# A cross-attention and mixture-of-experts layer: routed tiles in pairs, with a split down projection

## The reference

```python
x = x + xattn(layernorm(x), k, bias, ctx, ctx, num_heads=8)   # causal convolution over the features, per head
n = layernorm(x).reshape(2048, 256)
scores = softmax(n @ Wg.T)                                    # 16 experts in 4 groups
# the 2 best groups, then the 4 best experts of them; combine = their scores
h = silu(einsum('td,eid->eti', n, W1)) * einsum('td,eid->eti', n, W3)     # 176 hidden features
y = einsum('etd,te->td', einsum('eti,edi->etd', h, W2), combine)
z = (silu(n @ Ws1.T) * (n @ Ws3.T)) @ Ws2.T                   # shared expert, 352 hidden
out = x + y + z
```

## Time and profile before

| | |
|---|---|
| median of 3 runs | 452.86 us (450.76 to 453.48) |
| the profiled execution | 448.65 us, span 446.9 us |
| TensorE matmul (PE) busy | 420.3 us, 94% |
| VectorE (DVE) busy | 231.1 us, 52% |
| ScalarE (ACT) busy | 178.7 us, 40% |
| POOL busy | 185.3 us, 41% |
| chain that ended last | PE 83%, DMA 6%, DVE 3%, issue 3% |
| granted TensorE clock, mean | 0.996 |

### The profile page before, as it was taken

One profiled execution on the slowest core, in us unless ns is written; L12 is line 12 of the kernel. 1 busy time (PEld: TensorE's weight loads), 2 busy tenths in 40 slices (PEclk: granted clock), 3 DMA queues, 4 the chain that ended last, 5 costly groups with the idle time before them and its releaser, 6 DMA issues.

```text
span 446.9 us, 9516 instructions
## 1 busy us (share of the span) xinstructions
PE 420.3 (94%) x2197; PEld 303.5 (68%) x2198; DVE 231.1 (52%) x635; ACT 178.7 (40%) x522; POOL 185.3 (41%) x232
## 2 busy tenths in 40 slices
PE   0799999999899999998899999999999998999797
PEld 0678778877678455655666777777777776676576
DVE  2457668988877557384324343343333333333275
ACT  4335656644554531110243443444444443444221
POOL 3125233254887667752033333433433333333240
PEclk9999999999999999999999999999999999999989
DMA  7989999889989356544223333333333332334998
GB/s 196 271 214 245 232 231 226 229 205 273 306 233 319 139 163 244 200 172 149 55 93 105 100 112 113 109 115 100 111 114 103 109 112 89 111 100 126 338 385 312
DMA packets 47497, 79.97 MB, mean 179 GB/s; under 512 B 6017, under 2 KB 37233, under 8 KB 45425
## 3 DMA queue, kind: packets, MB, share of 16 engines
q1 hardware_dynamic: 40560, 59.74, 48.3%
q0 software_dynamic: 6912, 19.93, 11.4%
HBM read 55.12 MB, written 24.55 MB: 178 GB/s over the span
## 4 chain that ended last, share of the span: by engine, by line
PE 83%; DMA 6%; DVE 3%; issue 3%; ACT 2%; POOL 1%; DVEq 1%; POOLq 0%; ACTq 0%
PE heads L1120 19%; PE bank L1177 14%; PE heads L1032 11%; PE heads L1155 9%; PE heads L1034 6%; PE bank L1167 5%; PE heads L1130 4%; DMA y_scratch<-toep,dest_i 4%; PE bank L1143 3%; PE bank L1046 3%; PE bank L1239 2%; DMA ctx_n<-ctx_in 2%; PE bank L1057 2%; PE bank L1073 1%; DVE kv L639 1%
## 5 line engine op out<-in xcount | busy, mean ns | idle before, releaser
L622 POOL DMA_INDIRECT y_scratch<-toep,dest_i x80 | 77.5, 969 | 151.7 <-ACT toep L469 138.0
L1120 PE MATMUL heads<-w,toep 128*128 x320 | 111.1, 469 | 2.2 <-ACT toep L457 1.1
L1177 PE MATMUL bank<-w,toep 88*128 x320 | 83.5, 384 | 0.0
L1032 PE MATMUL heads<-toep,kv 128*128 128x256 f32 x256 | 79.8, 394 | 2.8 <-DVE kv L639 2.8
L1120 PEld LDWEIGHTS heads<-w,toep 128*128 128x128 f32 x320 | 56.7, 190 | 33.7 <-issue 12.0
L927 DVE COPY toep<-toep 128x1 f32 x77 | 11.8, 154 | 120.2 <-DMA y_scratch<-toep,dest_i 115.8
L571 POOL DMA_INDIRECT rows_scratch<-rows,slot_i x64 | 62.9, 983 | 21.6 <-issue 20.2
L1177 PEld LDWEIGHTS bank<-w,toep 88*128 88x128 f32 x320 | 54.9, 191 | 5.0
L653 DVE TENSOR_TENSOR prod<-heads,ctx_rep 128x1024 f32<-128x1024 f32 x32 | 39.2, 1224 | 30.0 <-PE heads L1034 29.6
L1034 PEld LDWEIGHTS heads<-toep,kv 128*128 128x128 f32 x256 | 49.8, 195 | 7.1
L463 ACT ACTIVATE toep<-heads 128x176 f32<-128x176 f32 x80 | 25.4, 317 | 71.3 <-PE heads L1120 71.3
(11 more groups left out here) (188 smaller groups left out, 454.5 us busy)
## 6 DMA issues: line engine op xcount, KB each, us to landing
ctx_rep<-ctxr_in SPq DMA_DIRECT2D x16, 1024.0 KB, 7.5
toep<-rows_scratch SPq DMA_DIRECT2D x77, 144.0 KB, 2.1
w<-w_in SPq DMA_DIRECT2D x16, 352.0 KB
w<-w_in SPq DMA_DIRECT2D x16, 176.0 KB
rows_scratch<-pad_row SPq DMA_DIRECT2D x17, 144.0 KB, 1.8
ctx_tr<-ctxt_in SPq DMA_DIRECT2D x16, 128.0 KB, 7.6
ctx_n<-ctx_in SPq DMA_DIRECT2D x16, 128.0 KB
toep<-kpad_scratch SPq DMA_DIRECT2D x4, 512.0 KB, 8.0
```

Source lines behind the costliest of these rows:

```text
L622: pool.indirect_dma_start(y_d, bass.IndirectOffsetOnAxis(ap=dest_i[b][:, 0:1].bitcast(U32), axis=0), y_sb[b], None).then_inc(y_sent[b], 16)
L1032: nc.tensor.matmul(y_ps[par][:, i, :], kv[:, q, 0, h * P:(h + 1) * P], toep[:, q * HH + h, :], start=True, stop=False)
L1120: last = nc.tensor.matmul(up_ps[p], x_tr[p][:, blk, :], w13[:, bass.ds(e, 1), blk, :].rearrange("p a n -> p (a n)"), start=blk == 0, stop= ...
L1177: last = nc.tensor.matmul(dn_ps[p], hid_tr[p][:, c, :], w2[:, bass.ds(e, 1), c, :].rearrange("p a n -> p (a n)"), start=c == 0, stop=c == 1)
```

## The change

Tiles go in pairs (p is the pair, q the tile in it, h the half of the buffers, 40 pairs). The hidden 176 features are split 128 + 48. hidden writes the 48s of both tiles side by side into one block of 128 columns, at 0 and at 64, so that three transposes turn a pair's hidden over (before four). down multiplies each tile's 128 features with the first block of w2, and then the two 48s, which lie on partitions 0 to 47 and 64 to 111, each on its own half of the array's rows and into its own PSUM bank. The 48 rows of w2 of each tile's expert must be on those partitions: w2 in DRAM is laid out with 128 partitions and two copies of its last 48 rows (176 to 256 KB per expert), and VectorE copies the right one into `w2_lo` for each tile (copy_w2). hidden, its PSUM and SBUF turned forms and the PSUM of turned rows are single now. VectorE takes gate and destination in one copy, and the destination is put where POOL reads it by places_of, which has the wait for `y_sent`; take has none. Within a step TensorE's order is up, turn_x, up, down of the pair before, turn_h of this pair.

Outside that loop: toep comes ready from the host instead of through kpad; the expert loads in the unit loop are gone, and twelve are made behind it; the activation table is loaded ahead; ScalarE and POOL do unit 0 before unit 1; TensorE does 40 transposes of the identity before its first work.

```diff
-HI = INTER // 2
+HI = P
+LO = INTER - P
+HALF = 64
...
+WARM_UP = 40
...
+TP = TILES // 2
+RING = TP // 2
+HID = (((0, INTER, 0),), ((0, P, 2 * P), (P, INTER, P + HALF)))
...
-w2 = sb("w2", [HI, E, 2, L])
+w2 = sb("w2", [P, E, 2, L])
...
-x_tr = [carve(L).rearrange("p (b n) -> p b n", b=LB) for _ in range(2)]
-act1 = [carve(INTER) for _ in range(2)]
-hid = [carve(INTER) for _ in range(2)]
-hid_tr = [carve(2 * P)[0:HI, :].rearrange("p (b n) -> p b n", b=2) for _ in range(2)]
+x_tr = [carve(2 * L).rearrange("p (q b n) -> p q b n", q=2, b=LB) for _ in range(2)]
+hid_tr = carve(3 * P).rearrange("p (c n) -> p c n", c=3)
 y_sb = [carve(L) for _ in range(DEPTH)]
-gate_c = [carve(2) for _ in range(DEPTH)]
+picked = carve(2 * DEPTH).rearrange("p (b i) -> p b i", i=2)
+act1 = [skip[:, i, 0:INTER] for i in range(2)]
+hid = vc[:].rearrange("p q n -> p (q n)")
+w2_lo = v
...
-ht_ps = [bank[i][0:HI, 0:2 * P].rearrange("p (b n) -> p b n", b=2) for i in (2, 3)]
+ht_ps = bank[2][:, 0:3 * P].rearrange("p (c n) -> p c n", c=3)
 dn_ps = [bank[i][:, 0:L] for i in (4, 5)]
-xt_ps = [bank[i][:, 0:L].rearrange("p (b n) -> p b n", b=LB) for i in (6, 7)]
+xt_ps = bank[6].rearrange("p (q b n) -> p q b n", q=2, b=LB)
...
-    for t in range(2 * DEPTH):
-        step(t, t % DEPTH, t // DEPTH)
-    with eng.Fori(2, TILES // DEPTH - 1) as it:
-        for b in range(DEPTH):
-            step(it * DEPTH + b, b, it)
-    for b in range(DEPTH):
-        step(TILES - DEPTH + b, b, TILES // DEPTH - 1)
+    for p in range(4):
+        step(p, p % 2, p // 2)
+    with eng.Fori(2, RING - 1) as it:
+        for h in range(2):
+            step(it * 2 + h, h, it)
+    for h in range(2):
+        step(TP - 2 + h, h, RING - 1)
...
+            sp.dma_start(toep[:, h:h + HH // 2, :], toep_d[:, h:h + HH // 2, :]).then_inc(toep_in[2 * q + part], 16)
+
+    load_x(0, 2, x_in[0])
+    load_tr(0)
     load_toep(0)
+    load_n(0)
     load_rep(0)
...
-        elif u < 12:
-            load_expert(u - 3 - (u > 6) - (u > 10), w_in)
...
-    with sp.Fori(EARLY, E - LATE) as e:
+    with sp.Fori(0, E - LATE) as e:
         load_expert(e, w_in)
...
-    def gather(t, b, before):
-        if tail_tile(t):
-            at = sp.value_load(tile_row[0:1, t:t + 1], min_val=0, max_val=E * REGION)
-            sp.dma_start(rows[:, b, :], rows_d[bass.ds(at, P)]).then_inc(tail_in[b], 16)
-            return
-        if not (isinstance(t, int) and t < DEPTH):
-            sp.wait_ge(xtr_ps, t - (DEPTH - 1))
-            sp.wait_ge(dest_ready, t - (DEPTH - 1))
-        at = sp.value_load(tile_row[0:1, bass.ds(t, 1)], min_val=0, max_val=E * REGION)
-        sp.dma_start(xg[b], rows_d[bass.ds(at, P)]).then_inc(rows_in[b], 16)
+    def gather(p, h, before):
+        if not (isinstance(p, int) and (p < 2 or p == TP - 1)):
+            sp.wait_ge(xtr_ps, p - 1)
+            sp.wait_ge(taken, p * 2 - 2)
+        for q in range(2):
+            t, b = p * 2 + q, 2 * h + q
+            at = sp.value_load(tile_row[0:1, bass.ds(t, 1)], min_val=0, max_val=E * REGION)
+            if tail_tile(t):
+                sp.dma_start(rows[:, b, :], rows_d[bass.ds(at, P)]).then_inc(tail_in[b], 16)
+            else:
+                sp.dma_start(xg[b], rows_d[bass.ds(at, P)]).then_inc(rows_in[b], 16)
...
+    nc.scalar.preload_act_table(ACT.Identity)
     act.wait_ge(const, C_IDENT)
-    moments1(0)
-    moments1(1)
     for u in range(2):
+        moments1(u)
         shift1(u)
         norm1(u)
...
+    def silu(p, q):
+        act.wait_ge(up_done, p * 2 + (q + 1))
+        if not (isinstance(p, int) and p < 1):
+            act.wait_ge(hid_ready, p * 2 + (q - 1))
+        nc.scalar.activation(act1[q], up_ps[q][:, 0:INTER], ACT.Silu).then_inc(silu_done, 1)
...
+    def store_y(p, h, before):
+
+        act.wait_ge(dn_done, p + 1)
+        for q in range(2):
+            at_least(act, y_sent[2 * h + q], before * 16)
+            nc.scalar.activation(y_sb[2 * h + q], dn_ps[q], ACT.Copy).then_inc(y_ready, 1)
...
+    def routed_step(p, h, before):
+        silu(p, 0)
+        if not (isinstance(p, int) and p == TP - 1):
+            src_tr(p + 1, 1 - h)
+        silu(p, 1)
+        if not (isinstance(p, int) and p == 0):
+            store_y(p - 1, 1 - h, before if h == 1 else before - 1)
...
+    def send(p, b):
+
+        pool.wait_ge(dest_ready, p + 1)
+        pool.wait_ge(y_ready, p * 2 + (b % 2 + 1))
         part(pool)
...
+    def hidden(p, q, b):
+
+        dve.wait_ge(silu_done, p * 2 + (q + 1))
+        if not (isinstance(p, int) and p == 0):
+            dve.wait_ge(ht_done, p)
+        dve.wait_ge(taken, p * 2 + (q + 1))
+        for lo, hi, at in HID[q]:
+            last = nc.vector.scalar_tensor_tensor(hid[:, at:at + hi - lo], act1[q][:, lo:hi], picked[:, b, 0:1],
+                                                  up_ps[q][:, INTER + lo:INTER + hi], ALU.mult, ALU.mult)
+        last.then_inc(hid_ready, 1)
+
+    def copy_h(p):
+        dve.wait_ge(ht_done, p + 1)
+        if not (isinstance(p, int) and p == 0):
+            dve.wait_ge(dn_done, p)
+        nc.vector.tensor_copy(hid_tr, ht_ps).then_inc(htr_ready, 1)
+
+    def copy_w2(p, q, h, e):
+
+        if not (isinstance(p, int) and p < 2):
+            dve.wait_ge(dn_done, p - 1)
+        at = slice(q * HALF, q * HALF + LO)
+        nc.vector.tensor_copy(w2_lo[at, h, :], w2[at, bass.ds(e, 1), 1, :].rearrange("p a n -> p (a n)")
+                              ).then_inc(w2lo_ready, 1)
+
+    def places_of(p, h, before):
+
+        for q in range(2):
+            at_least(dve, y_sent[2 * h + q], before * 16)
+        nc.vector.tensor_copy(dest_i[:, 2 * h:2 * h + 2], picked[:, 2 * h:2 * h + 2, 1]).then_inc(dest_ready, 1)
...
-            dve.wait_ge(y_sent[b], before * 16)
         e = dve.value_load(tile_e[0:1, bass.ds(t, 1)], min_val=0, max_val=E - 1)
-        nc.vector.tensor_copy(gate_c[b][:, 0:1], src[:, bass.ds(e + L, 1)]).then_inc(gate_ready, 1)
-        nc.vector.tensor_copy(dest_i[b][:, 0:1], src[:, bass.ds(e + (L + E), 1)]).then_inc(dest_ready, 1)
+        nc.vector.tensor_copy(picked[:, b, :].unsqueeze(2),
+                              src[:, L:].rearrange("p (i e) -> p i e", e=E)[:, :, bass.ds(e, 1)]
+                              ).then_inc(taken, 1)
+        return e
...
+    def routed_step(p, h, before):
+        experts = [take(p * 2 + q, 2 * h + q, before) for q in range(2)]
+        hidden(p, 0, 2 * h)
+        for q in range(2):
+            copy_w2(p, q, h, experts[q])
+        hidden(p, 1, 2 * h + 1)
+        places_of(p, h, before)
+        copy_h(p)
...
+    for _ in range(WARM_UP):
+        nc.tensor.transpose(y_ps[1][:, 0, 0:P], ident[:], ident[:])
...
-    def turn_h(w, p):
-        pe.wait_ge(hid_ready, w + 1)
-        if not (isinstance(w, int) and w < 2):
-            pe.wait_ge(htr_ready, w - 1)
-        for c in range(2):
-            last = nc.tensor.transpose(ht_ps[p][:, c, :], hid[p][:, c * HI:(c + 1) * HI], ident[:])
+    def turn_h(p):
+        pe.wait_ge(hid_ready, p * 2 + 2)
+        if not (isinstance(p, int) and p == 0):
+            pe.wait_ge(htr_ready, p)
+        for c, at in enumerate((0, 2 * P, P)):
+            last = nc.tensor.transpose(ht_ps[:, c, :], hid[:, at:at + P], ident[:])
         last.then_inc(ht_done, 1)
...
+    def down(p, h):
+        if not (isinstance(p, int) and p == 0):
+            pe.wait_ge(y_ready, p * 2)
+        pe.wait_ge(htr_ready, p + 1)
+        pe.wait_ge(w2lo_ready, p * 2 + 2)
+        for q in range(2):
+            e = pe.snap(expert_of[2 * h + q], min_val=0, max_val=E - 1)
+            nc.tensor.matmul(dn_ps[q], hid_tr[:, q, :], w2[:, bass.ds(e, 1), 0, :].rearrange("p a n -> p (a n)"),
+                             start=True, stop=False)
+        for q in range(2):
+            at = slice(q * HALF, q * HALF + LO)
+            last = nc.tensor.matmul(dn_ps[q], hid_tr[at, 2, :], w2_lo[at, h, :], start=False, stop=True)
...
+    def routed_step(p, h, before):
+        up(p, 0, h)
+        if not (isinstance(p, int) and p == TP - 1):
+            turn_x(p + 1, 1 - h, before + h)
+        up(p, 1, h)
+        if not (isinstance(p, int) and p == 0):
+            down(p - 1, 1 - h)
+        turn_h(p)
```

More of the change, by code:

```diff
@@ L56 @@
 KEEP_WARM = 16
+WARM_UP = 40
 LATE = 4
-EARLY = 7
 PAIRS = (0, 3, 6, 9, 12)
@@ L156, in build @@
                  for mem in (wide_rep[:, 2560:2560 + 3 * GT * P], kv_flat[:, 0:3 * GT * P])]
-        dest_i = [sb(f"dest_i{i}", [P, 1], I32) for i in range(DEPTH)]
+        dest_i = sb("dest_i", [P, DEPTH], I32)
         def fin_in_memory(mem, at, n):
@@ L986, in _ @@
             add_z(15)
-            def routed_step(t, b, before):
-                take(t, b, before)
-                if not (isinstance(t, int) and t == 0):
-                    copy_h(t - 1, 1 - b % 2)
-                hidden(t, b % 2, b)
+            def routed_step(p, h, before):
[6 more added lines that the diff above has]
+                copy_h(p)
             routed(dve, routed_step)
```

(30 more changed lines are left out.)

120 lines of the change are left out of this document (34 added, 86 removed).

## The result

The changed kernel takes 456.92 us (median of 4 runs, 455.35 to 457.16), the kernel before, on the same chip, 451.81 (449.67 to 453.48): ratio 1.0138, 95% interval 1.0093 to 1.0183. It is 1.4% slower, where 3% less was forecast. The profiled execution took 455.35, its span is 453.6, 6.7 more than before.

A forecast was written before the change was run, and what follows sets the result against it. SyncE's gather, not TensorE, was taken as the likely bound, at 4.9 us a pair. Gains of 10.4 (loop), 2.5 (start) and 1.0 (unit loop), 13.9 together, took 448.65 to 434.8 us, 439 as a median; range 428 to 450.

The forecast's parts named there:

- 4.57 + 0.14 = 4.71: TensorE's work on a pair in the routed loop: 4.57 us, plus 0.14 for going in and out of the parts.
- rival (2): Routed loop: the two 48s do not overlap, 5.14 us a pair, 449 us in all (451 with the old stall); chance 0.12.
- Path (b): Routed loop, from a send's landing through places_of, takes and SyncE's gather to turn_x: three steps take 14.8 us, 4.93 a pair.
- The cover of turn_h: End of a step: hidden is ready 2.45 us after the second up began, TensorE free after 2.48, so cover just enough.
- The start, 2.5 us: Before the units: earlier table load, VectorE's new order and warm-up transposes together gain 2.5 us, bounds -2 and +3.5.
- Rival (3): Start: the 40 transposes run slow and do not warm the clock, the convolution starts at 14.0, also slow; 444 us, chance 0.09.
- The unit loop, 1.0: Unit loop: freed DMA time may remove a TensorE wait of 1.49 us at 117; 1 us gained, bounds 0 and 1.5.
- Weights cost nothing: Behind the units: twelve experts' loads, 7.3 MB, take 19 us to about 152, where DMA is little used; no cost.
- reads 10 us behind step 36 and 34 before the end: Tail: the reads of y come again some 10 us behind step 36 and 34 us before the end.
- Rival (4): Send loop: each landing takes 1.6 us more as two sends follow each other; 5.47 us a pair, 459 us, chance 0.07.

The follow-up runs named there:

- the fastest version: Changed kernel with VectorE's takes ahead of copy_h and TensorE's register loads a pair ahead: 457.33 us, ratio 0.9897 to the kernel before; again 457.41 us, 0.9873.
- the version with the start alone: Kernel before with the changed kernel's start and order of loads, w2 and routed loop in the old form: 460.2 us, ratio 0.9949 to the kernel before.
- the version with both edits and no parts: Changed kernel with early takes, register loads a pair ahead, and the 48s one after the other on the whole array: 446.38 us, ratio 0.9934 to the kernel before.

## Why the prediction was wrong, step by step

The forecast for the profiled execution was 434.8; it took 455.35, 20.5 more. Of these 18.0 are the loop (10.4 gained was forecast, 7.6 lost), 1.6 the start and the units (3.5 against 1.9), 1.0 the tail.

- *"I take 4.57 + 0.14 = 4.71"*: wrong, the term for the parts was mis-sized. The shared 48s take 0.63 + 0.48 with the transposes behind them; the forecast had 0.43 + 0.33 + 0.14 = 0.90. The 0.21 is 7.6 us in 36 pairs. The likely reason, not tested: the nearest row, L1046, held four parts of which eight instructions followed each other, so what it costs to get in and out was spread over eight; and I counted the 48s at the full 2:1. That parts do run at once was right (0.63 is less than 0.86), and rival (2) had the right direction. The Trainium skill's rule that I weighed (TensorEngine Tiling (Array Packing), Key Properties: a change of mode drains) fits in sign: the 0.15 more on the transposes stands right behind the parts, and is absent in the chain without parts. No run measures a drain by itself.
- *"Path (b) ... three steps take 14.8: 4.93 us a pair"*: wrong in its shape. I hung it on the send's landing, over three steps. In fact VectorE's places_of waits little for sends in the changed kernel (4.9 us in 120), and the cycle, read in the version with TensorE's loads a pair ahead, runs over two steps through turn_h, copy_h and the takes, 10.3 us. The two takes cost 1.9 us from the end of copy_h, not 1.35 but the upper bound, since the loop's branch and two register loads of 0.30 lie in the open; and the parts' 0.21 stands in this cycle too. 5.15 a pair instead of 4.93 is 7.9 us. My guess that SyncE's gather would bound the pair was right once TensorE's loads were out of the way, and the path through the send comes back in the fastest version, where rows are late.
- *The cover of turn_h, 2.45 against 2.48, "without it some 0.1 to 0.2 a pair"*: wrong, and here is the step that I did not see at all. The engine does not idle ahead of turn_h (0.0 in 120 us), but I counted TensorE's queue at nothing. Behind a wait, even one of a few hundredths, stand a register load of 0.30 and an up that takes 0.26 more. Most of it comes behind the wait for rows at turn_x (3.5 of 5.4 us), the rest behind turn_h at the loop's branch (1.9); moving turn_h away left 5.0. The remaining 5.40 - 5.15 = 0.25 a pair, 9.0 us, is this; making the loads a pair ahead alone gives 7.8, doubling them costs about as much.
- *The start, 2.5 us*: the size was nearly right (1.9; 2.8 at the first up in the version with the start alone), one cause wrong. The warm-up's half microsecond is nothing: without it the time is the same. Rival (3) spoke of the transposes not warming the clock: they do (below), but in the profiled execution the clock fell back 1.2 us after the pause of kv_blocks.
- *The unit loop, 1.0*: nothing came of it. The first skip_sum is 2.15 us earlier and the first up 1.9.
- *Weights cost nothing; reads 10 us behind step 36 and 34 before the end*: right (10.1 and 34.8).
- Rival (2) left out the 1.0 of the unit loop, so its 449 should be 448. Rival (4) named 459 for a pair of 5.47. The time was near, the mechanism was not: the sends are not what is late.

The three terms of the loop, 7.6, 7.9 and 9.0, do not simply add to the 18.0, since TensorE's sum and the gather's cycle stand beside each other and the parts' 0.21 is in both. The forecast and all its rivals gave the loop a single bound and left out how one queue's stall feeds the next. What keeps the fastest version at 5.0 instead of 4.7 is for the larger part the parts' own 0.21, and for the rest rows that come late.

## What to carry to other kernels

Before moving a wait on a queue, list what stands right behind it: register loads, address arithmetic and weight loads that the queue used to do in advance come into the open, and a wait of 0.03 us cost 0.58 here. Follow each cycle between engines by its own instructions and count how many steps it spans by the buffer that closes it, before dividing by that number. And for two parts of an array that only two products share, do not count on the ideal saving until a run of that shape has been measured: here it was 0.08 us of 0.43.

## What the runs showed of the hardware

- Two products of 48 rows on two row parts take 0.63 us where full-array products of the same columns take 0.86, and the next three transposes 0.48 instead of 0.33: 0.08 us saved. The timeline of the weight loads shows one thing that may explain it: ahead of the parts and of the transposes behind them they start only after 0.33 us of idle time, with the products; on the full array, in the version with both edits and no parts (last row), they follow each other. Whether the chip or the order of the instructions asks for that was not tried.

```profile
320.43 0.30 PEld L1201 LDWEIGHTS bank<-v,toep 48*128 48x128 f32 x4 [0.33 <-issue]
321.06 0.31 PEld L1147 LDWEIGHTS heads<-ident,vc 128*128 128x128 f32 x3 [0.33 <-issue]
...
325.86 0.47 PEld L1158 LDWEIGHTS heads<-ident,vc 128*128 128x128 f32 x3
```

- Transposes do raise the clock here: the chain of the changed kernel's start has 40 of them, then first convolutions at the time of the fast level and later ones at that of the slow one. Behind it a window of the same kernel (its granted clock is the third number from the end), and the first convolution in the timeline without the transposes.

```profile
1.87 6.18 PE heads L1109 x40
...
11.71 0.44 PE heads L1046 x2
...
12.58 0.85 PE heads L1046 x2
...
12.00:13.00 1.00, 1.00 (x5) 0.91 (x4) 0.00 (x0) 0.26 (x1) 0.00 (x0) 0.50 1.03 203
...
10.10 1.19 PE L1046 MATMUL heads<-toep,kv 128*128 128x256 f32 x2 [2.55 <-DVE kv L634]
```

  The first 16 transposes start 0.21 to 0.27 us apart, the others 0.11 to 0.14. Then TensorE idles for 2.55 us of kv_blocks, starts fast (0.44), is slow from 12.0 to 15 us (granted clock 0.50, 0.85 for the pair that took 0.44), and fast again from the first skip_sum at 16.84 on. In the profile of the same kernel on the other chip the transposes take 7.54 us, the convolutions start at 12.18 and all are fast (0.43), and the first skip_sum comes at 16.74; so when the clock rises and whether it falls back differs between executions. Without the transposes the convolutions start slow (two of them, 1.19 and 1.06 us in the timeline, against 0.67 and 0.61 with them), are fast from 13.56 on, and slow again at 17 to 20 us (granted clock 0.50). The Trainium skill (TensorE: Matmul & The Clock Gate, Part 4) says that the fast clock does not engage for transposes; for these, of fp32 data, it did in both profiles, and the measurement decides.
- Where the kernel before took 462 us, all ten profiles, its own among them, have one stall of ScalarE of 15.0 to 17.2 us in the shared stage (nine are put down to "remote", another core or an unknown queue, one to TensorE), and the profiles where it took 449 to 452 don't. It is most of the difference between chips: the first up of the kernel before comes 13.2 us later there, and the span is 13.8 longer. No record names what it waits for.
